# Attention and mixture-of-experts kernel: order of the first tiles, permuted normalised rows, gate and up weights in 4 KB runs

## What is computed

```python
x = x + xattn(ctx, layernorm(x))      # similarity of context rows, top 30 % kept, symmetrised, times gamma
x = x + ffn(layernorm(x))             # layernorm of the 2048 rows, then:
    scores = sigmoid(h @ router_w)    # 32 experts; 4 of 8 groups, then 8 experts of 32, per row
    routed = sum over the row's 8 experts of share * (silu(h @ w_gate[e]) * (h @ w_up[e])) @ w_down[e]
    shared = (silu(h @ sw_gate) * (h @ sw_up)) @ sw_down
```

## Time and profile before

| | us |
|---|---|
| median of three runs | 998.78 (994.36 to 998.79) |
| the profiled execution | 1004.59 |
| its span, first to last instruction | 1002.9 |
| mean granted clock of PE | 0.955 of full speed |
| PE busy | 895.2 (89 %) |
| DVE busy | 571.9 (57 %) |
| ACT busy | 501.8 (50 %) |
| POOL busy | 452.1 (45 %) |

### The profile page before, as it was taken

The page is one execution under the profiler, slowest core; times in us unless marked ns, Lnnn a source line. Parts: engine busy times, 40 slices in busy tenths (PEclk is TensorE's granted clock), DMA queues, the critical chain, the costliest instruction groups (busy, mean ns, idle before and its releaser), DMA issues.

```text
span 1002.9 us, 21954 instructions
## 1 busy us (share of the span) xinstructions
PE 895.2 (89%) x4596; PEld 476.9 (48%) x4597; DVE 571.9 (57%) x1261; ACT 501.8 (50%) x995; POOL 452.1 (45%) x348
## 2 busy tenths in 40 slices
PE   4267788878978999999999999999999999999984
PEld 1143444435434555555555555555554555555542
DVE  5878999888883444346444444445445455363321
ACT  4486473853323455455544554455546465464331
POOL 1131121220142466555647554756545665656642
PEclk8579799999998999999999999999999999999998
DMA  4122030111447787878787887878787888877754
GB/s 156 42 81 79 27 113 2 43 46 42 158 144 223 172 187 137 186 175 242 178 214 151 174 204 178 181 175 183 181 227 183 233 192 222 195 179 130 146 94 76
DMA packets 90267, 149.25 MB, mean 149 GB/s; under 512 B 9648, under 2 KB 46768, under 8 KB 90224
## 3 DMA queue, kind: packets, MB, share of 16 engines
q0 software_dynamic: 33120, 80.64, 40.0%
q1 hardware_dynamic: 57104, 68.13, 21.1%
HBM read 101.55 MB, written 47.20 MB: 148 GB/s over the span
## 4 chain that ended last, share of the span: by engine, by line
PE 54%; DMA 6%; issue 5%; ACT 2%; POOL 2%; DVE 2%; ACTq 1%; DVEq 1%; SPq 0%; POOLq 0%
PE bank L259 46%; PE bank L1507 5%; DMA stage_dn<-in_L_ffn_w_down_dram 4%; PE bank L1498 3%; DMA out_dram<-y,ids_i 3%; POOL out_dram L1217 1%; ACT gu L241 1%; ACTq L1174 1%; DVEq L1174 1%; DVE gu L248 1%; DVE dn L251 0%; POOL s_hT L315 0%; DVE hid L1407 0%; POOLq L1174 0%; SPq L231 0%
## 5 line engine op out<-in xcount | busy, mean ns | idle before, releaser
L259 PE MATMUL bank<-gu,xgT 128*128 x1764 | 405.7, 380 | 1.5 <-DVE xgT L1399 1.0
L1217 POOL DMA_INDIRECT out_dram<-y,ids_i x145 | 237.0, 1635 | 241.6 <-DMA out_dram<-y,ids_i 130.4
L1399 DVE TENSOR_TENSOR xgT<-bank,xgT 128x512 f16<-128x512 f32 x148 | 102.3, 691 | 292.0 <-ACT xgT L1260 240.6
L259 PEld LDWEIGHTS bank<-gu,xgT 128*128 128x128 f16 x1764 | 172.7, 98 | 178.3 <-issue 3.5
L259 PE MATMUL bank<-dn,hT 128*128 x870 | 213.0, 381 | 0.6
L1205 POOL DMA_INDIRECT xg<-xrows,ids_i x153 | 164.7, 1077 | 71.7 <-issue 44.2
L1260 ACT CAST xgT<-bank 128x512 f16<-128x512 f32 x148 | 86.7, 586 | 131.4 <-issue 111.4
L1285 ACT ACTIVATE y<-bank 128x512 f32<-128x512 f32 x145 | 87.1, 601 | 117.3 <-PE bank L259 90.7
L259 PEld LDWEIGHTS bank<-dn,hT 128*128 128x128 f16 x870 | 85.2, 98 | 75.6 <-issue 8.3
L1266 ACT ACTIVATE silu<-bank 128x256 f32<-128x256 f32 x147 | 56.1, 381 | 99.8 <-PE bank L259 83.5
L1407 DVE SCALAR_TENSOR_TENSOR hid<-bank,xg,silu 128x256 f32<-128x256 f32 x147 | 70.6, 480 | 59.7 <-ACT silu L1266 57.3
(11 more groups left out here) (220 smaller groups left out, 775.8 us busy)
## 6 DMA issues: line engine op xcount, KB each, us to landing
stage_gu<-in_L_ffn_w_gate_dram SPq DMA_DIRECT2D x32, 512.0 KB
stage_gu<-in_L_ffn_w_up_dram SPq DMA_DIRECT2D x32, 512.0 KB
stage_dn<-in_L_ffn_w_down_dram SPq DMA_DIRECT2D x32, 512.0 KB
x_sb<-in_x_dram SPq DMA_DIRECT2D x4, 1024.0 KB, 7.3
xrows<-adj SPq DMA_DIRECT2D x4, 1024.0 KB, 4.2
out_dram<-acc SPq DMA_DIRECT2D x4, 1024.0 KB, 4.7
xg<-xrows,ids_i POOLq DMA_INDIRECT x153
out_dram<-y,ids_i POOLq DMA_INDIRECT x145
```

What stands on the lines that cost most here:

```text
L259: last = nc.tensor.matmul(out_ap, stationary(a, c), moving(w, c), start=(c == 0 and (a, w) == parts[0]), stop=(c == chunks - 1 and (a, w) ...
L1217: g_.indirect_dma_start(out, bass.IndirectOffsetOnAxis(ap=ids_i[:, t:t + 1], axis=0), y[:, t % YS, :], None, compute_op=ALU.add).then_inc( ...
L1399: v.tensor_tensor(xgT[:, s, 1, :, :], bank[XB[s]][:, :].rearrange("p (k t) -> p k t", k=KC), xgT[:, s, 0, :, :], ALU.subtract).then_inc(S[ ...
```

## The change

The permutation: number 4q+c of a normalised row is written to place 128c+q. Chunk c of the row then holds the numbers 4q+c, so partition q of a weight matrix holds the rows 4q to 4q+3, which for an expert's gate and up are 4 KB in one run of DRAM. The staging buffer is laid out to match, and its conversion pieces are gate and up in place of two chunks of both. The router's weights and the shared gate and up are laid out in the same way (the shared ones still come in runs of 1 KB, since a load takes half of the columns). The order of the first tiles changes on PE, ACT and DVE.

```diff
         def gu_slot(n, part, piece):
             if isinstance(n, int):
-                return gu16[:, n % WS, part, 2 * piece:2 * piece + 2, :].rearrange("p k n -> p (k n)")
-            return gu16[:, bass.ds(n % WS, 1), part, 2 * piece:2 * piece + 2, :].rearrange("p a k n -> p (a k n)")
+                return gu16[:, n % WS, part, :, piece * I:(piece + 1) * I]
+            return gu16[:, bass.ds(n % WS, 1), part, :, piece * I:(piece + 1) * I].rearrange("p s k i -> p (s k) i")
...
         def stage_gu(n, piece):
             if isinstance(n, int):
-                t = stage["first_gu"][:, 2 * piece:2 * piece + 2, :, :] if n < SH else stage["gu"][:, n % 2, 2 * piece:2 * piece + 2, :, :]
-                return t.rearrange("p k a i -> p (k a i)")
-            return stage["gu"][:, bass.ds(n % 2, 1), 2 * piece:2 * piece + 2, :, :].rearrange("p s k a i -> p (s k a i)")
+                return stage["first_gu"][:, :, piece, :] if n < SH else stage["gu"][:, n % 2, piece, :, :]
+            return stage["gu"][:, bass.ds(n % 2, 1), piece, :, :].rearrange("p s k i -> p (s k) i")
...
-            sp.dma_start(stage["first_gu"][:, :, 0, :], sw_gate[:, c].rearrange("(k p) i -> p k i", p=P)).then_inc(arrived, 16)
-            sp.dma_start(stage["first_gu"][:, :, 1, :], sw_up[:, c].rearrange("(k p) i -> p k i", p=P)).then_inc(arrived, 16)
+            sp.dma_start(stage["first_gu"][:, :, 0, :], sw_gate[:, c].rearrange("(p k) i -> p k i", p=P)).then_inc(arrived, 16)
+            sp.dma_start(stage["first_gu"][:, :, 1, :], sw_up[:, c].rearrange("(p k) i -> p k i", p=P)).then_inc(arrived, 16)
...
-            gu, dn = stage["gu"][:, parity], stage["dn"][:, parity]
-            sp.dma_start(gu[:, :, 0, :], g.rearrange("(k p) i -> p k i", p=P)).then_inc(S["weights_loaded"], 16)
-            sp.dma_start(gu[:, :, 1, :], u.rearrange("(k p) i -> p k i", p=P)).then_inc(S["weights_loaded"], 16)
-            sp.dma_start(dn[:, :, :], d.rearrange("(k p) h -> p k h", p=P)).then_inc(S["weights_loaded"], 16)
...
+            sp.dma_start(gate, g.rearrange("(p k) i -> p k i", p=P)).then_inc(S["weights_loaded"], 16)
+            sp.dma_start(up, u.rearrange("(p k) i -> p k i", p=P)).then_inc(S["weights_loaded"], 16)
+            sp.dma_start(dn, d.rearrange("(k p) h -> p k h", p=P)).then_inc(S["weights_loaded"], 16)
...
-                sp.dma_start(rw[:, :, :], router_w.rearrange("(k p) e -> p k e", p=P)).then_inc(S["small_loaded"], 16)
+                sp.dma_start(rw[:, :, :], router_w.rearrange("(p k) e -> p k e", p=P)).then_inc(S["small_loaded"], 16)
...
-                        t = v.tensor_scalar(xn[:, i, :], acc[:, b * RT + i, :], mv[:, 0, i, 0:1], rs[:, 0, i:i + 1],
+                        t = v.tensor_scalar(xn[:, i, :].rearrange("p (c q) -> p q c", c=KC),
+                                            acc[:, b * RT + i, :].rearrange("p (q c) -> p q c", c=KC), mv[:, 0, i, 0:1], rs[:, 0, i:i + 1],
                                             ALU.subtract, ALU.mult)
...
-        stage["gu"] = sb("stage_gu", [P, 2, KC, 2, I])
+        stage["gu"] = sb("stage_gu", [P, 2, 2, KC, I])
...
-                def step(t, i):
+                def step(t, i, early=False, late=False):
...
                     split_rows(t + 2, s)
-                    next_weights(fresh, e)
+                    if late:
+                        next_weights(info_of(act, 1, t - 1), info_of(act, 0, t - 1))
+                    if not early:
+                        next_weights(fresh, e)
                     gates(t + 1, 1 - s)
                     hidden(t, s)
...
-                    step(t, (t + 2) % YS)
+                    step(t, (t + 2) % YS, t == 0, t == 1)
...
                 pe.wait_ge(S["added"], TT - 3)
                 rows_T(0, 0, 0)
+                s_down(pe, b, RT - 1)
                 pe.wait_ge(S["added"], TT - 2)
                 rows_T(1, 1, 1)
-                s_down(pe, b, RT - 1)
                 pe.wait_ge(S["tables_ready"], 1)
```

More of the change, by code:

```diff
@@ L228, in load @@
             sp.wait_ge(S["weights_loaded"], done)
-            gu, dn = stage["gu"][:, parity], stage["dn"][:, parity]
-            sp.dma_start(gu[:, :, 0, :], g.rearrange("(k p) i -> p k i", p=P)).then_inc(S["weights_loaded"], 16)
-            sp.dma_start(gu[:, :, 1, :], u.rearrange("(k p) i -> p k i", p=P)).then_inc(S["weights_loaded"], 16)
-            sp.dma_start(dn[:, :, :], d.rearrange("(k p) h -> p k h", p=P)).then_inc(S["weights_loaded"], 16)
+            if isinstance(parity, int):
+                gate, up, dn = stage["gu"][:, parity, 0, :, :], stage["gu"][:, parity, 1, :, :], stage["dn"][:, parity, :, :]
+            else:
+                gate, up = (stage["gu"][:, bass.ds(parity, 1), a, :, :].rearrange("p s k i -> p (s k) i") for a in range(2))
+                dn = stage["dn"][:, bass.ds(parity, 1), :, :].rearrange("p s k h -> p (s k) h")
+            sp.dma_start(gate, g.rearrange("(p k) i -> p k i", p=P)).then_inc(S["weights_loaded"], 16)
+            sp.dma_start(up, u.rearrange("(p k) i -> p k i", p=P)).then_inc(S["weights_loaded"], 16)
+            sp.dma_start(dn, d.rearrange("(k p) h -> p k h", p=P)).then_inc(S["weights_loaded"], 16)
         def convert_high(act, n):
@@ L1424, in _, with step @@
                 gates(0, 0, 0, info_of(dve, 0, 0))
-                def step(t, x):
+                def step(t, x, early=False, late=False):
                     s = x % 2
@@ L1430, in step @@
                     split_rows(t + 2, s)
-                    next_weights(fresh, e)
+                    if late:
+                        next_weights(info_of(dve, 1, t - 1), info_of(dve, 0, t - 1))
+                    if not early:
+                        next_weights(fresh, e)
                     gates(t + 1, 1 - s, (x + 1) % XG, next_e)
@@ L1435, in _ @@
                 for t in range(2):
-                    step(t, t)
+                    step(t, t, t == 0, t == 1)
                 with dve.Fori(2, PLAIN - XG + 1, XG) as t:
```

## The result

The changed kernel takes **1011.80 us** (median of 4 runs, 1009.37 to 1017.47), the kernel before 998.09 beside it (4 runs, 994.36 to 998.79): a ratio of 1.0127 with an interval of 1.0085 to 1.0168. It is slower by about 13 us, above the range of 991 to 1006. The profiled execution took 1009.37 us, span 1007.6, against 1004.59 and 1002.9 before. One execution of the kernel before beside e5 to e8 took 3267.66 us and is left out.

A forecast was written before the change was run, and what follows sets the result against it. It took TensorE to bound the steady tiles and nearly full DVE the attention stage. Terms -5.1 + 2.0 + 3.2 - 0.5 = -0.4 us, carried to the median of 998.78, gave 998.4 us, range 991 to 1006.

The forecast's parts named there:

- part 3's path: Attention stage: the permuted write of normalised rows lengthens DVE's work, which TensorE awaits in every batch: +3.2 us (0 to +10.5).
- the new wait at the seam: Seam between the stages: TensorE waits 2.9 us before its third transposes, with a clock loss of +2.0 us (0 to 2.4).
- the upper end of +10.5: Permuted write in the attention stage: upper bound if DVE's elements cost ACT's 1.83 ns, +0.70 us per instruction.
- The sign that the prediction had named for itself: Prediction is wrong if the attention stage changes by more than 5 us or TensorE waits in the steady stage.
- Parts 1 and 2: Seam: moved conversion and moved shared down product together start tile 1's hidden transposes earlier, -5.1 us at full clock.
- Part 1: Seam: expert 2's conversion moves behind tile 1's gates; the product that started at 314.12 starts 6.0 us earlier.
- rival (c): Seam: weights or ACT late, TensorE waits 2 to 3 us at tile 2's hidden transposes; about +3, 1002; within the 0.55.
- the cover of 0.7 us: Seam: DVE gates tile 2 by 310.9, TensorE asks at about 311.6; a miss costs some tenths.
- Part 2: Seam: the last shared down product goes ahead of tile 1's transposes, filling a 1.50 us wait but losing 0.9 us.
- Part 4: Loads: gate and up come in 4 KB runs instead of 1 KB; -0.5 us (0 to -3.5).
- (b): Attention stage, four batches: strided write costs DVE what it costs ACT; sum +6.9, 1005.7 us; shares the 0.20 for slower.
- a case in which the stride costs nothing: Permuted write: DVE keeps its two-port mode at any stride, so the write adds nothing; by that alone the sum is -3.6.

The follow-up runs named there:

- e5: Changed kernel with twelve identity transposes, result unread, on PE ahead of its wait for the normalised rows: 1012.88 us, ratio 1.0130.
- e8: Kernel before with an unused DVE addition of 250 columns (0.42 us per batch) ahead of the normalised rows' writes: 1001.69 us, ratio 1.0001.
- e4: Kernel before with an unused DVE addition of 640 columns (0.82 us per batch) ahead of its contiguous writes: 1010.23 us, ratio 1.0088.
- e6: Changed kernel with the normalised rows announced tile by tile, so PE transposes the first while DVE writes the second: 1003.34 us, ratio 1.0045.
- e9: Changed kernel with the shared expert's last down group moved ahead of PE's wait for the normalised rows: 1006.65 us, ratio 1.0048.
- e10: Changed kernel with the shared expert's last down group moved between the rows' transposes and the router: 1005.82 us, ratio 1.0049.
- e15: Kernel before with only expert 2's weight conversion moved behind the early tiles: 999.57 us, ratio 0.9978.
- e12: Kernel before with only gate and up loaded in 4 KB pieces and converted in the new layout (results wrong): 1000.41 us, ratio 1.0005.
- e2: Changed kernel without its new order at the seam, so permutation and 4 KB runs only: 1010.68 us, ratio 1.0072.
- e13: Kernel before with rows announced by tile, expert 2's conversion moved, and the last shared down group between transposes and router: 1000.28 us, ratio 0.9997.
- e1: Kernel before with only the change of order at the seam, both parts of it: 1000.65 us, ratio 0.9983.

## Why the prediction was wrong

**The step that failed is part 3's path, +3.2 us.** Its first half held nearly: 0.78 us forecast for one permuted write, 0.807 measured; 0.96 us more of DVE per batch reckoned, 0.73 to 0.75 measured, about 3 us in all. But the text carried these on to the end one for one, and priced the clock only behind the new wait at the seam. In the attention stage the same engine waited in the same way, behind the wait stand matmuls that PE runs at either clock, and the row of the clock was at hand. There 3 us of DVE became 10.8 us of start 2. e4 shows that lateness alone does it; e6, e9 and e10 show that more than half of the loss goes when the router of the later batches runs at or near 2.4 GHz though the write stays as dear. The text also took DVE for the engine that sets the pace to the end, "none in batch 3" of idle time. But the trace of before has DVE waiting 1.40 us for PE's down product behind batch 3's rows (249.17), so PE's speed was already on the path there, and that wait became 5.89. The term that should have stood in the sum is, from e4, +8.6 (medians) to +10.2 (start 2, 274.6 against 264.4); the upper end of +10.5 covered the size, but for another cause (DVE at ACT's rate), so it was set apart as a rival with a small chance. With +8.6 to +10.2 here and the 0 that the seam gave, the sum comes to +8 to +10 us; the last 3 to 5 of the measured 13 belong to no term that a run shows. The sign that the prediction had named for itself did come: the attention stage changed by more than 5 us.

**The bound that was missing.** The clock behind the seam's new wait was taken at +2.0 and was 0 in the changed kernel (2.76 us for twelve behind 2.39 of waiting). In e5 it was paid, and +2.0 was about its size:

```profile
310.54 1.11 PE L1519 MATMUL bank<-ident,xg 128*128 128x128 f32 x4 [2.81 <-DVE acc L323]
311.57 5.23 PE L262 MATMUL bank<-gu,xgT 128*128 x12
```

In the five other kernels with this order it was not, one of them with nearly the same wait (e10, 2.75 us). So the term was a possibility and not a certainty, and the place I left out paid. An estimate from rows 6 alone, by the length of the wait, could not have told this: e5's 1.36 us lost the clock and the seam's 2.39 did not. What makes the clock fall in one execution and hold in another stays open. What I could have had was a bound: the router's and the down group's difference between the two levels, 3.2 + 2.6 us, for each batch, and the question where DVE has nothing else to do meanwhile. Only batch 3 came near it.

**Parts 1 and 2, -5.1 and then +2.0.** The profiled execution gave -1.9, the middle of all executions 0. Part 1 alone did what its steps said up to the fourth product (e15). Then came rival (c), a wait of 1.6 to 2.7 us at tile 2's hidden transposes in every run with the new order; the cover of 0.7 us was too thin, as the text feared, but it had this at "some tenths". Part 2 lost 1.8 us by the same middles and not 0.9. And the stall in the one profile of before, 3.87 us, was the worst of six executions with that order (1.17 to 2.33 in the others), so part of the gain was never there to be won.

**Part 4, -0.5.** e12 gives 1.0005 (0.9979 to 1.0030), in line with it and with 0. In the changed kernel q1's packets fell from 57104 to 32144, its busy share from 21.1% to 20.6%.

**Rivals.** (b) came out on the right side and near the right time, but by a mechanism that did not happen: no write took 1.1 us. What remains open is why kernels with the permuted write and a mostly fast router (e6, e9, e10) stay 0.45 to 0.49% above the kernel before. e12 leaves the pieces at most 0.3%; DVE's 3 us are the obvious term, but no run isolates them, since any delay moves the clock as well. The profiles of these three are among their fastest executions, so they may show less of it than there is: the mean granted clock of all executions has a median of 0.949, 0.947 and 0.950 there, against 0.952 before and 0.937 in e2 and e4.

**The pages.** The write's factor is 0.807 / 0.541 = 1.49. The Trainium skill (Advanced Engine Details and Errata, SBUF Cachelines) has an access that goes to another line each time pay a penalty; the trace agrees in direction. The conditions of the mode in the Trainium skill (VectorE: DVE Perf Modes, What auto-detection actually checks) name no stride for fp32, from which the prediction had a case in which the stride costs nothing; that case did not come, and no run shows which mode the engine was in. For the clock, the Trainium skill reports (TensorE: Matmul & The Clock Gate, A second HAM failure mode) another kernel in which frequent idle moments between groups of matmuls make the clock swing. The trace has such moments ahead of half-speed matmuls, 0.95 us of waiting and a pause of 0.73 in e12's batch 3; but before's batch 3 has 2.10 and 0.73 and kept its clock, so that they are the cause here isn't shown.

## What to carry to other kernels

At every wait of TensorE that a change lengthens, however little, look at what stands behind it: the same matmuls timed at both clocks give the bound of the loss. Then ask whether another engine has work meanwhile; where it has none, the bound is nearly the price. If the work behind the wait is small (transposes, narrow matmuls), try to hand the rows over in smaller portions (e6), or to put a full-width group ahead of the narrow one (e9, e10), before trying to shorten the wait. The second delays what the narrow matmuls feed, and where the clock wasn't what cost, it gave nothing (e13). And compare a stall with those of other executions before counting its removal as gain.

## What the runs showed of the hardware

- The router's 32 fp32 matmuls of 32 columns stayed at 1.2 GHz for all of their 6.9 us, with PE almost never idle (5.93 of 6.00 us from 127 to 133). In e10 the clock came back within twelve fp16 ones of 512 columns (3.57 us; 5.31 at 1.2 GHz, 2.75 at 2.4).
- TENSOR_SCALAR on 128 x 512 fp32 takes 0.541 us contiguously, 0.733 with a read step of 16 bytes and 0.807 with a write step of 512. Four in a row span 1.91, 2.68 and 2.66 us.
- The last tiles run slower than the steady 4.54 us per tile, by an amount that changes from one execution to the next. Over the last eight it adds up to 7.4 us in before, 6.8 in e1, 6.1 in e2 and 3.2 to 3.9 in after, e4, e8, e10 and e12. PE's timeline of before has pauses there that no semaphore ends:

```profile
947.10 0.63 PE L1507 MATMUL bank<-ident,xg 128*128 128x128 f32 x4 [0.58 <-issue]
...
952.59 0.63 PE L1507 MATMUL bank<-ident,xg 128*128 128x128 f32 x4 [0.72 <-issue]
```

  It follows neither the order nor the pieces and can mask a change of 4 us in a pair of traces: the spans of before and after differ by 4.7 us, start 2 by 10.8.
